# A mixed-kernel convolution: the last image's kernel is mixed by GpSimd instead of VectorE

## The reference, cut to what matters

```python
gap = x.mean((2, 3))
cw = jnp.maximum(gap @ w1.T, 0.0) @ w2.T
pooled = x.reshape(b, c, POOL, h // POOL, POOL, w // POOL).mean((3, 5))
cp = pooled.mean(1).reshape(b, POOL * POOL)
ew = cp @ w_exp.T
routing = jax.nn.sigmoid(cw[:, :, None] * ew[:, None, :])
combined = jnp.einsum('bik,koiuv->boiuv', routing, weight)
# then: image b is convolved with combined[b], 3x3, padding 1, and added to x
```

## Time and profile before

| what | value |
|---|---|
| time, median of three runs | 1807.97 us (1805.74 to 1810.24) |
| profiled execution, first to last instruction | 1807.2 us |
| mean granted PE clock of it | 0.970 |
| busy: PE / DVE / ACT / POOL | 1678.7 / 1077.2 / 966.8 / 871.1 us |
| mixed-kernel convolution on PE | 478.00 to 512.06 us of the span |

### The profile page before, as it was taken

How to read it: one execution, slowest core, us unless ns; L and a number is a source line. 1 busy time by engine, 2 the same in 40 slices (tenths; PEclk the granted TensorE clock), 3 DMA queues, 4 the chain that set the end, 5 groups by cost and what they waited for, 6 DMA issues and landing times. The chain is left out here.

```text
span 1807.2 us, 32921 instructions
## 1 busy us (share of the span) xinstructions
PE 1678.7 (93%) x12503; PEld 955.4 (53%) x12503; DVE 1077.2 (60%) x1532; ACT 966.8 (53%) x1427; POOL 871.1 (48%) x730
## 2 busy tenths in 40 slices
PE   5879999999689999998999997999999769999998
PEld 3635555554244444444444445777777535555554
DVE  6667777766863332365334236666656467777766
ACT  2545555555236666526666645666666355555554
POOL 3318887877025333313333335333323008877777
PEclk8999999999799999998999998999999879999999
DMA  5004343333202222401222340000000004333333
GB/s 126 1 15 118 108 111 111 110 109 101 74 1 79 90 83 66 103 2 32 93 79 67 96 95 1 1 2 1 2 1 1 3 5 122 116 118 116 114 116 103
DMA packets 74948, 121.64 MB, mean 67 GB/s; under 512 B 18306, under 2 KB 22594, under 8 KB 74146
## 3 DMA queue, kind: packets, MB, share of 16 engines
q1 hardware_dynamic: 74786, 119.48, 22.7%
HBM read 115.74 MB, written 3.67 MB: 66 GB/s over the span
## 5 line engine op out<-in xcount | busy, mean ns | idle before, releaser
L766 POOL TENSOR_TENSOR x<-x,mx_gated 128x512 f32<-128x512 f32 x254 | 326.7, 1286 | 85.6 <-DVE mx_gated L718 83.4
L711 DVE TENSOR_TENSOR mx_hidden<-ps,mx_hidden 128x1024 f32<-128x1024 f32 (+1 forms) x256 | 246.2, 962 | 177.2 <-PE ps L579 176.7
L579 PE MATMUL ps<-tokens_high,w_high 64*128 64x512 f32 x1536 | 330.9, 427 | 8.7 <-ACT mx_hidden L873 5.0
L873 ACT ACTIVATE mx_hidden<-ps,w_bias 128x1024 f32<-128x1024 f32 x256 | 264.1, 1115 | 124.8 <-PE ps L579 124.8
L579 PE MATMUL ps<-tokens_high,w_low 64*128 64x512 f32 x1536 | 305.7, 393 | 0.0
L579 PE MATMUL ps<-tokens_low,w_high 64*128 64x512 f32 x1536 | 305.5, 393 | 0.0
L919 POOL TENSOR_TENSOR x<-x,mx_gated 128x512 f32<-128x512 f32 x126 | 161.5, 1282 | 253.3 <-DVE mx_gated L891 253.3
L891 DVE SCALAR_TENSOR_TENSOR mx_gated<-ps,w_bias,mx_gates 128x512 f32<-128x512 f32 x128 | 96.0, 750 | 280.1 <-PE ps L843 260.6
L694 ACT ACTIVATE mx_hidden<-ps 128x1024 f32<-128x1024 f32 x256 | 248.5, 1022 | 15.4 <-PE ps L579 1.4
L1884 DVE TENSOR_TENSOR c_near_weights<-c_near_hats 128x768 f32<-128x768 f32 x192 | 190.0, 1037 | 102.8 <-PE ps L1755 102.8
L648 PE MATMUL ps<-mx_hidden,w_second 128*64 128x512 f32 x1024 | 248.4, 605 | 0.4 <-DVE mx_hidden L711 0.4
(11 more groups left out here) (225 smaller groups left out, 1905.6 us busy)
## 6 DMA issues: line engine op xcount, KB each, us to landing
mx_gates<-gate_board SPq DMA_DIRECT2D x768, 128.0 KB, 3.1
w_first<-in_f_first SPq DMA_DIRECT2D x4, 1024.0 KB, 11.6
c_weight<-in_c_weight SPq DMA_DIRECT2D x1, 2304.0 KB
x<-in_x SPq DMA_DIRECT2D x8, 256.0 KB, 5.8
w_second<-in_f_second SPq DMA_DIRECT2D x4, 512.0 KB, 13.3
w_first<-in_f_first SPq DMA_DIRECT2D x4, 512.0 KB, 9.8
out_x<-x SPq DMA_DIRECT2D x16, 128.0 KB, 2.7
gate_board<-xn SPq DMA_DIRECT2D x56, 16.0 KB, 2.1
```

Source lines behind the costliest of these rows:

```text
L579: last = pe.matmul(out[h], weights[w][half(h), w_own], tokens[t][half(h), t_own], start=(p == 0), stop=(p == 2))
L711: dve.tensor_tensor(own, second[:, 0:halves, :], own, ALU.mult).then_inc(s.hidden.semaphore, 1)
L766: pool.tensor_tensor(place, place, gated[:, n % GATED, :], ALU.add).then_inc(s.added.semaphore, 1)
L873: act.activation(hidden[:, n % HIDDEN, f], first[:, (n * F + f) % BLOCKS], ACT.Gelu, bias=w.bias1[:, e * F + f:e * F + f + 1]).then_inc(s. ...
```

## The change

For the last image (j=3) DVE's `mix` is left out. POOL does it: as soon as `weight` is loaded (`k.fetched_sem`) and `routing` is there, it multiplies expert 0's kernel by its routing into a new tile `last_mixed`, and then for each of the other seven experts multiplies into a second new tile `last_part` and adds that to `last_mixed`; the last sum goes to `kernel[:, 3]`. Each of the 15 instructions waits for the one before. PE waits for a new semaphore ahead of image 3, and POOL's `split_weights` follows, now after three kernels from DVE.

```diff
+        last_mixed, last_part = sb("last_mixed", [P, KERNEL]), sb("last_part", [P, KERNEL])
...
         @block.gpsimd
         def _(pool):
             pool.memset(padded[:], 0.0).then_inc(s.cleared, 1)
-            pool.wait_ge(s.kernel, IMAGES)
+            j = IMAGES - 1
+            pool.wait_ge(k.fetched_sem, k.fetched)
+            pool.wait_ge(s.routing, 1)
+            pool.tensor_scalar(last_mixed[:], weight[:, 0], routing[:, j, 0:1], None, ALU.mult).then_inc(s.last_mixed, 1)
+            for e in range(1, EXPERTS):
+                pool.wait_ge(s.last_mixed, 2 * e - 1)
+                pool.tensor_scalar(last_part[:], weight[:, e], routing[:, j, e:e + 1], None, ALU.mult).then_inc(s.last_mixed, 1)
+                pool.wait_ge(s.last_mixed, 2 * e)
+                to = last_mixed[:] if e < EXPERTS - 1 else kernel[:, j]
+                pool.tensor_tensor(to, last_mixed[:], last_part[:], ALU.add).then_inc(s.last_mixed, 1)
+            pool.wait_ge(s.kernel, IMAGES - 1)
             split_weights(k, pool)
...
             for j in range(IMAGES):
                 pe.wait_ge(s.padded, j + 1)
-                pe.wait_ge(s.kernel, j + 1)
+                if j < IMAGES - 1:
+                    pe.wait_ge(s.kernel, j + 1)
+                else:
+                    pe.wait_ge(s.last_mixed, 2 * EXPERTS - 1)
...
             for j in range(IMAGES):
-                mix(j)
+                if j < IMAGES - 1:
+                    mix(j)
                 if j >= 2:
                     add(j - 2)
```

More of the change, by code:

```diff
@@ L2358, in __init__ @@
         self.kernel = new("c1_kernel")
+        self.last_mixed = new("c1_last_mixed")
         self.out_ps = new("c1_out_ps")
```

## The result

The changed kernel takes 1815.24 us, the median of six runs (1814.24 to 1816.46), against 1807.97 us for the kernel before, the median of five (1804.80 to 1810.24): a ratio of 1.0041, with a 95% interval of 1.0030 to 1.0052. A sixth execution of the kernel before took 3347.35 us and is left out here. Slower by 0.4%, then, as forecast (1815.2), and inside the range. The profiled span went from 1807.2 to 1812.4 us.

What follows compares the result with a forecast made beforehand. TensorE bounds the kernel, in this stage waiting only for the first mixed kernel. DVE delays of 5.2 and 6.4 us make 11.6, less 4.4 slack: 7.2 added to 1807.97 gives 1815.2 us, range 1808.5 to 1821.0.

Steps and rivals of the forecast that it cites:

- the delay of DVE: Mixing of images 0 and 1: POOL's turns make the first kernel 5.2 us late and image 1's 11.6.
- the slack: Convolution, image 1: its kernel is ready 4.4 us before PE asks for it.
- the clock's 1.7: Convolution: PE's second wait may drop the clock to 0.50 for 3.4 us, costing 1.7; only in the range.
- Nothing is gained by taking image 3 from DVE.: Image 3's mix, about 6.5 us on DVE, is covered by PE's matmuls; removing it was costed at nothing.
- Each POOL instruction holds up a DVE instruction.: Mixing, images 0 and 1: each POOL instruction delays one DVE instruction by its own duration less 0.26 us hidden.
- The 1.16 for a tensor_tensor: Mixing: DVE's delay per POOL tensor_tensor, 1.42 us less 0.26 hidden.
- The 0.43 for a tensor_scalar: Mixing: DVE's delay per POOL tensor_scalar, 0.69 us less 0.26 hidden.
- "I take 0.69": POOL's tensor_scalar on 128x576, priced at 0.69 us from a cast of 0.613 us for 512 columns.
- rival B: POOL's tensor_scalar is as dear as a tensor_tensor, all 15 costing DVE 1.16 us: 1821.0 us; chance 0.13.
- The Trainium skill's rule: Shared SBUF port: the second engine is blocked for the first's whole instruction, nothing hidden; loss 11.0 us.
- Rival A: Mixing: POOL gets no turn until DVE's adds, so its kernel comes late; loss 0 to 2.9 us; chance 0.17.
- rival C: Convolution faster through less DVE work; only a shorter low-clock stretch, at most 3 us; chance 0.08 including the unseen.

Runs made afterwards that it cites:

- The copies: Changed kernel with GpSimd's eight tensor_scalar replaced by plain copies of the same size, last image's routing left out: 1813.06 against 1808.37 us, ratio 1.0030.
- chain unused: Kernel before, all four kernels still mixed by VectorE, plus GpSimd's 15 instructions whose result nobody reads: 1814.72 against 1806.93 us, ratio 1.0040.

## Why the prediction was right

The sign, the size and the cause were right: the two engines take turns, and the first kernel is what PE waits for. That the forecast of 1815.2 was met so closely is luck. Three terms were off and nearly cancelled: the delay of DVE was 1.2 us too large in the sum (11.6 against 10.4), the slack 1.3 too small (4.4 against 5.7), and the clock's 1.7 stood in the range only.

- *Nothing is gained by taking image 3 from DVE.* Right: 0.9996 when only that was done.
- *Each POOL instruction holds up a DVE instruction.* Right, and shown by adding them without use, by taking them out of DVE's way, and by putting memsets in their place. In the changed kernel six of the seven tensor_tensors cost a scalar_tensor_tensor 1.02 us (1.84 against 0.82), the other a DVE tensor_scalar 1.13, and the eight tensor_scalars 0.36 each; with 0.24 on one more DVE tensor_scalar that is 10.4 us, where the count gave 11.6. The 1.16 for a tensor_tensor was a little dear. The 0.43 for a tensor_scalar was near, but for no good reason: by the rule that gave it, the duration less 0.26, an instruction of 1.72 us would cost 1.46.
- *"I take 0.69" for POOL's tensor_scalar: the step that failed.* It is 1.72 us. By the prediction's own sign ("over 1 us of its own") this was rival B. B's condition came true: one tensor input did not make it cheap, it is longer than the two-input tensor_tensor (1.40). But B's price, 1821.0, did not: B expected a dear one to hold DVE longer, and it holds a scalar_tensor_tensor for 0.36 us, less than a tensor_tensor does. Its length did something else: it spread the turns over three images, and POOL was done at 502.26, not before 497. So the first kernel was late by 2.1 us, not 5.2; image 1's by 6.4, not 11.6; and image 2's, which was to be in time, by 10.4. The copies, whose length alone was not measured but which are shorter than the tensor_scalar by about 1.0 us beside DVE (1.07 against 2.11), give the picture nearly as it was drawn.
- *Where the slack breaks.* It was to break at image 1 (11.6-4.4=7.2). It broke at image 2: its slack was 496.5-490.67-0.15=5.7 us, and 10.4-5.7=4.7. The clock, which stood in the range and not in the forecast, added 1.7: 6.4, with 6.6 measured in the stage.
- *The Trainium skill's rule* ("SBUF — State Buffer", Who interferes with whom) is borne out on who meets whom: DVE's instructions with two SBUF inputs meet POOL's reads (1.84 us beside a tensor_tensor) and not its writes (0.82 beside the memsets). That DVE's tensor_scalar meets writes too fits what the page says of DVE's 2-port modes, though no run here shows that it was in one. On "the whole instruction", which the page says of those modes and the prediction applied to all, the rows differ by POOL's operation. A scalar_tensor_tensor that met a tensor_tensor ended 0.62 us behind that one's end, all six times (502.87 behind 502.26): it was kept to the end, and yet 1.02 us were lost, not 1.40. One that met a tensor_scalar was done before that one was (492.43, under way until 492.80), and lost 0.36 of 1.72. There the measurement decides.
- *Rival A*, POOL shut out by DVE's quick succession: it was not. POOL's own waits were 0.08 to 0.10 us, under the 0.8 from which it would have decided. Its other end, PE waiting for POOL, needs a later start: 7.29 us when POOL began behind the second kernel. What *rival C* allowed for, a shorter low stretch of the clock, came (4.32 us in place of 6.00), but PE then waited 0.64 us for image 1's kernel, so most of it was lost again.

## What to carry to other kernels

Work moved from VectorE to GpSimd is not always moved out of VectorE's way: the two meet at reading SBUF, and not at semaphores alone. Ask first which of VectorE's instructions meet it; here those with two SBUF inputs and the tensor_scalar did, the adds with one input in PSUM did not. Then count it by turns, one delay for each GpSimd instruction, and charge it to whatever VectorE is doing that is urgent at that moment, not to what it was relieved of. Before moving work off an engine, ask which of its instructions the bound engine waits for; here it was the first kernel alone, and cutting that in two gained 1.8 us, where GpSimd's help lost 7.3 and ScalarE's could not be told from none. And price an operation on an engine by that operation: the price of a neighbour, scaled to the same shape, was wrong by 2.5 times.

## What the hardware showed that was not expected

GpSimd's tensor_scalar on 128x576 takes 1.72 us alone, more than its tensor_tensor with two inputs (1.40), and only some 0.07 of that is the scalar read from memory (2.04 with a constant against 2.11, both beside VectorE). It keeps a scalar_tensor_tensor of VectorE waiting for only a fifth of its length. VectorE's own tensor_scalar did not get away so early: the one that came upon it ended 0.31 us behind its end (493.11 behind 492.80), as another did behind a tensor_tensor's (483.30 behind 482.99). Why the two kinds differ was not tried. VectorE's tensor_scalar, unlike its scalar_tensor_tensor, is slowed by GpSimd's memsets (0.52 to between 0.66 and 0.98 us). The clock fell behind idle times of 2.48 us (changed kernel) and 2.50 us (chain unused), as after 2.49 us in the earlier trace rows, and stayed at 1.00 behind the 2.13 us of the copies.
